# Token stage of an audio tower: the pointwise convolution an iteration later, four accumulator banks for it and two for the convolution, the second norm one iteration behind the first

## The reference, cut to what matters

```python
# token stage, for each of 16 batches: x is 64 channels x 2048
h = conv1d(x, conv_in_w, stride=1, pad=3)                     # 64 -> 128 channels, 7 taps
h = gelu(groupnorm1(h, gn1_w, gn1_b))                         # norm over all of a batch
h = conv1d(h, dw_w, stride=2, pad=2, groups=H) + dw_b         # depthwise, 5 taps, 128 x 1024
h = conv1d(h, pw_w)                                           # pointwise, 128 -> 128
h = gelu(groupnorm1(h, gn2_w, gn2_b))                         # 16 x 128 tokens of 1024
# then h + attention(layernorm(h)), then + mixture of low-rank experts on layernorm(...)
```

## Time and profile before

| | |
|---|---|
| median of three runs | 2040.95 us |
| profiled execution | 2044.69 us |
| its span | 2042.9 us |
| PE busy | 1892.5 us, 93% |
| DVE busy | 1321.2 us, 65% |
| ACT busy | 773.2 us, 38% |
| POOL busy | 308.4 us, 15%, all but 83 us of it before 421 us |

### The profile page before, as it was taken

The page is one execution under the profiler, slowest core; times in us unless marked ns, Lnnn a source line. Parts: engine busy times, 40 slices in busy tenths (PEclk is TensorE's granted clock), DMA queues, the critical chain, the costliest instruction groups (busy, mean ns, idle before and its releaser), DMA issues. The chain is left out here.

```text
span 2042.9 us, 32412 instructions
## 1 busy us (share of the span) xinstructions
PE 1892.5 (93%) x11538; PEld 1029.6 (50%) x11538; DVE 1321.2 (65%) x2742; ACT 773.2 (38%) x2020; POOL 308.4 (15%) x596
## 2 busy tenths in 40 slices
PE   4898898559999999999999999999999999859999
PEld 2344444335555555555555555555555555425554
DVE  4678777436666666666666666666666666555554
ACT  3454554233333334433333433333343333332221
POOL 2376675300000000000000000000000000033332
PEclk9899999679999999999999999999999999979999
DMA  5244342332222322232222222223222222243332
GB/s 143 52 86 96 81 95 65 76 91 51 58 58 59 76 56 53 58 76 59 58 58 55 73 58 58 58 58 75 55 55 58 40 39 39 39 138 80 80 82 73
DMA packets 305609, 138.87 MB, mean 68 GB/s; under 512 B 295088, under 2 KB 295344, under 8 KB 303408
## 3 DMA queue, kind: packets, MB, share of 16 engines
q1 hardware_dynamic: 301136, 108.35, 24.8%
q10 hardware_dynamic: 4320, 28.51, 4.0%
HBM read 56.07 MB, written 8.39 MB: 32 GB/s over the span
## 5 line engine op out<-in xcount | busy, mean ns | idle before, releaser
L1031 PE MATMUL out_ps<-m_h,ot_h 128*128 128x512 f16 x1024 | 389.4, 380 | 1.7 <-DVE ot_l L835 1.7
L1032 PE MATMUL out_ps<-m_l,ot_h 128*128 128x512 f16 x1024 | 389.0, 380 | 0.0
L1033 PE MATMUL out_ps<-m_h,ot_l 128*128 128x512 f16 x1024 | 388.9, 380 | 0.0
L756 ACT ACTIVATE qp_h<-qp_ps 128x512 f16<-128x512 f32 x126 | 75.3, 597 | 492.6 <-PE qp_ps L966 492.6
L812 ACT ACTIVATE prob<-s_ps,nmx 128x128 f32<-128x128 f32 x512 | 181.3, 366 | 207.3 <-DVE nmx L905 207.3
L885 DVE SCALAR_TENSOR_TENSOR resid<-out_ps,resid 128x512 f32<-128x512 f32 x256 | 176.1, 688 | 97.1 <-PE out_ps L1033 97.1
L835 DVE SCALAR_TENSOR_TENSOR qp_l<-qp_ps,qp_h 128x512 f16<-128x512 f32 x126 | 87.2, 692 | 234.5 <-ACT qp_h L756 234.5
L1221 POOL MEMSET fpower<- 128x1 f32 x1 | 0.1, 99 | 1392.4 <-POOLq L674 1392.4
L966 PE MATMUL qp_ps<-lat,wp_h 128*128 128x512 f16 x756 | 205.6, 381 | 0.0
L1033 PEld LDWEIGHTS out_ps<-m_h,ot_l 128*128 128x128 f16 x1024 | 100.4, 98 | 121.6 <-issue 1.4
L1031 PEld LDWEIGHTS out_ps<-m_h,ot_h 128*128 128x128 f16 x1024 | 100.5, 98 | 110.5 <-DVE ot_l L835 2.7
(11 more groups left out here) (217 smaller groups left out, 3861.3 us busy)
## 6 DMA issues: line engine op xcount, KB each, us to landing
wide<-heads_in ACTq DMA_DIRECT2D x30, 928.0 KB, 4.7
wide<-x_in SPq DMA_DIRECT2D x30, 512.0 KB, 6.5
tower_out<-result SPq DMA_DIRECT2D x16, 512.0 KB, 2.6
stage<-wb_in SPq DMA_DIRECT2D x8, 512.0 KB, 8.3
resid<-wqk_in SPq DMA_DIRECT2D x1, 2304.0 KB, 11.6
zt<-z SPq DMA_TRANSPOSE x128, 2.4
turned<-halves SPq DMA_TRANSPOSE x128, 3.0
wide<-heads_in SPq DMA_DIRECT2D x2, 928.0 KB, 4.6
```

The lines of the kernel that those rows point to most:

```text
L756: act.activation(out, src, ACT.Copy, scale=scale).then_inc(done, 1)
L1031: pe.matmul(out_ps[hf][:, :], ot_h[:, h, :], m_h[:, at], start=h == 0, stop=False)
L1032: pe.matmul(out_ps[hf][:, :], ot_h[:, h, :], m_l[:, at], start=False, stop=False)
L1033: last = pe.matmul(out_ps[hf][:, :], ot_l[:, h, :], m_h[:, at], start=False, stop=h == HEADS - 1)
```

## The change

- The pointwise product gets a lag of its own, PW = 2. It moves from the end of PE's iteration to the place behind the statistics matmul, ahead of chunk 1. HID, PROJ and TAIL become 3, 4 and 5; LOW is merged into TAIL. The number of iterations stays the same.
- Banks: two for the convolution's chunks, four for the pointwise product (two batches of two halves). `stat_ps` becomes four columns of the second convolution bank, so the statistics matmul waits until that bank's chunk has been copied, and chunk 1 waits until the statistics have been copied.
- Tap 0 of the depthwise convolution goes from DVE to ACT, behind the first Gelu.
- ACT's order: chunks 0, 1 and 2 are copied, then the second Gelu, the first Gelu, tap 0, `x_high`, chunk 3, the latents' high parts, the squares.
- POOL's order: group norms, latent scales, layer norm, and `x_low` last.
- DVE's order: the pointwise product's statistics ahead of the taps, the latents' low parts at the end of the iteration.
- SP's order: the next x is loaded ahead of the latents' transposing DMAs.

```diff
-    AHEAD, MID, HID, PROJ, TAIL, LOW = -1, 1, 2, 3, 4, 5
+    AHEAD, MID, PW, HID, PROJ, TAIL = -1, 1, 2, 3, 4, 5
-        conv_ps = [pb("conv_ps0"), pb("conv_ps1"), pb("conv_ps2")]
-        stat_ps = pb("stat_ps")
-        pw_ps = [pb("pw_ps0"), pb("pw_ps1")]
+        conv_ps = [pb("conv_ps0"), pb("conv_ps1")]
+        pw_ps = [[pb(f"pw_ps{b}{hf}") for hf in range(2)] for b in range(2)]
+        stat_ps = conv_ps[1][:, 0:4]
...
@@ sync, body @@
-                if ok(LOW):
-                    b = i - LOW
+                if ok(-2) and i >= -1:
+                    sp.wait_ge(x_hi, i + 2)
+                    sp.wait_ge(x_lo, i + 2)
+                    load(i + 2, 0, XW, x_loaded)
+                if ok(TAIL):
+                    b = i - TAIL
                     sp.wait_ge(lat_lo, b * 2 + 2)
...
@@ scalar, body @@
+                if ok(TAIL) and i - TAIL + PROJ >= B:
+                    squares(i - TAIL)
                 if ok(0):
                     copy_y1(i, p, 0)
-                if ok(AHEAD):
-                    x_high(i - AHEAD)
-                if ok(0):
                     copy_y1(i, p, 1)
-                if ok(MID):
-                    act.wait_ge(gn_step, i * GN_STEPS)
-                    need(act, dw_step, (i - MID) * DW_TAPS, B * DW_TAPS)
-                    act.activation(g1[:, DW_PAD:DW_PAD + T], y1[1 - p][:, :], ACT.Gelu, bias=c12[:, 1:2],
-                                   scale=c12[:, 0:1]).then_inc(gelu1_done, 1)
-                if ok(0):
                     copy_y1(i, p, 2)
                 if ok(HID):
...
+                if ok(MID):
+                    b = i - MID
+                    act.wait_ge(gn_step, i * GN_STEPS)
+                    need(act, dw_step, b * DW_TAPS, B * DW_TAPS)
+                    act.activation(g1[:, DW_PAD:DW_PAD + T], y1[1 - p][:, :], ACT.Gelu, bias=c12[:, 1:2],
+                                   scale=c12[:, 0:1]).then_inc(gelu1_done, 1)
+                    act.wait_ge(gelu1_done, b + 1)
+                    need(act, pw_done, b * 2, 2 * B)
+                    act.activation(dw[:, :], g1[:, 0:2 * D:2], ACT.Identity, bias=params[:, 5:6],
+                                   scale=params[:, 0:1]).then_inc(dw_step, 1)
+                if ok(AHEAD):
+                    x_high(i - AHEAD)
                 if ok(0):
                     copy_y1(i, p, 3)
...
@@ gpsimd, body @@
-                if ok(AHEAD) and i >= 0:
-                    x_low(i - AHEAD)
                 if ok(TAIL):
                     latent_scales(i - TAIL)
                 if ok(HID):
                     layer_norm(i - HID)
+                if ok(AHEAD) and i >= 0:
+                    x_low(i - AHEAD)
...
@@ vector, body @@
-                if ok(LOW):
-                    latents_low(i - LOW)
...
                     stats1(i, p, 1)
-                if ok(MID):
-                    for k in range(DW_TAPS):
-                        tap(i - MID, k)
+                if ok(PW):
+                    b = i - PW
+                    for hf in range(2):
+                        dve.wait_ge(pw_done, b * 2 + (hf + 1))
+                        dve.bn_stats(bn2[:, hf, :], pw_ps[b % 2][hf][:, :]).then_inc(bn2_done, 1)
+                    wait_apart(dve, dve_passed, (bn2_done, b * 2 + 2), (stat_done, i))
+                    mean_and_square(st2_ready, b, st[:, 2:4], bn2[:, :, :])
                 if ok(HID):
...
+                if ok(0):
+                    stats1(i, p, 2)
...
+                if ok(MID):
+                    for k in range(1, DW_TAPS):
+                        tap(i - MID, k)
+                if ok(0):
                     stats1(i, p, 3)
...
+                if ok(TAIL):
+                    latents_low(i - TAIL)
...
@@ tensor @@
-                need(pe, y1_copied, i * 4 + (c - 2), 4 * B)
+                need(pe, y1_copied, i * 4 + (c - 1), 4 * B)
+                if c == 1:
+                    need(pe, s_copied, i, LAST + HID)
...
                     need(pe, s_copied, i - 1, LAST + HID)
-                    pe.matmul(stat_ps[:, 0:4], keep["mean_mat"][:, :], st[:, :], start=True, stop=True
+                    need(pe, y1_copied, i * 4, 4 * B)
+                    pe.matmul(stat_ps, keep["mean_mat"][:, :], st[:, :], start=True, stop=True
                               ).then_inc(stat_done, 1)
+                if ok(PW):
+                    pointwise(i - PW)
                 if ok(0):
                     conv(i, p, 1)
...
                 if ok(PROJ):
                     project(i - PROJ)
-                if ok(MID):
-                    pointwise(i - MID)
```

More of the change, by code:

```diff
@@ L179, in token_phase @@
         HEAD = 2 * CHUNK + 8
-        lags = list(range(AHEAD, LOW + 1))
+        lags = list(range(AHEAD, TAIL + 1))
         block = ctx.enter_context(nc.Block())
@@ L260, in copy_y1 @@
                     need(act, gelu1_done, i - 1, B)
-                act.activation(y1[p][:, c * CHUNK:(c + 1) * CHUNK], conv_ps[(i * 4 + c) % 3][:, :], ACT.Copy
+                act.activation(y1[p][:, c * CHUNK:(c + 1) * CHUNK], conv_ps[(i * 4 + c) % 2][:, :], ACT.Copy
                                ).then_inc(y1_copied, 1)
@@ L264, in copy_y1, with squares @@
                     weights_high("wqk", QUARTERS[c])
+            def squares(b):
+                act.wait_ge(proj_done, b + 1)
+                need(act, rms_step, b * RMS_STEPS, B * RMS_STEPS)
+                need(act, ss_done, b * 2, 2 * B)
+                act.activation(junk[:, :], q_ps[:, 0:QR], ACT.Square, scale=UN * QR ** -0.5,
+                               accum_out=ss[:, 0:1]).then_inc(ss_done, 1)
+                act.wait_ge(ss_done, b * 2 + 1)
+                act.activation(junk[:, 0:KVR], kv_ps[:, 0:KVR], ACT.Square, scale=UN * KVR ** -0.5,
+                               accum_out=ss[:, 1:2]).then_inc(ss_done, 1)
             def body(i, p, ok):
@@ L295, in body @@
                     for hf in range(2):
-                        act.activation(resid[:, b * D + hf * CHUNK:b * D + (hf + 1) * CHUNK], pw_ps[hf][:, :],
-                                       ACT.Gelu, bias=c12[:, 3:4], scale=c12[:, 2:3]).then_inc(gelu2_done, 1)
+                        act.activation(resid[:, b * D + hf * CHUNK:b * D + (hf + 1) * CHUNK],
+                                       pw_ps[b % 2][hf][:, :], ACT.Gelu, bias=c12[:, 3:4], scale=c12[:, 2:3]
+                                       ).then_inc(gelu2_done, 1)
+                if ok(MID):
[10 more added lines that the diff above has]
+                    x_high(i - AHEAD)
                 if ok(0):
@@ L308, in body @@
                                    ).then_inc(kc_hi, 1)
[L309 to L318, removed]
+                if ok(PROJ) and i < B:
+                    squares(i - PROJ)
             act.wait_ge(zeroed, ZEROED)
-            pipeline(act, body, -1, lags, LOW)
+            pipeline(act, body, -1, lags, TAIL)
         @block.gpsimd
@@ L432, in tap, with hid_low @@
             def tap(b, k):
[L434 to L443, removed]
+                dve.wait_ge(dw_step, b * DW_TAPS + k)
+                dve.scalar_tensor_tensor(out=dw[:, :], in0=g1[:, k:k + 2 * D - 1:2],
+                                         scalar=params[:, k:k + 1], in1=dw[:, :],
+                                         op0=ALU.mult, op1=ALU.add).then_inc(dw_step, 1)
+            def hid_low(b):
+                dve.wait_ge(hid_hi, b + 1)
+                need(dve, hid_turned, b * 16, B * 16)
+                low(hid2[:, D:2 * D], hid[:, :], LN_S, hid2[:, 0:D], hid_lo)
             def take_latents(b):
@@ L489, in body @@
                     need(dve, gn_step, (i - 1) * GN_STEPS, (LAST + HID) * GN_STEPS)
-                    dve.tensor_copy(s[:, :], stat_ps[:, 0:4]).then_inc(s_copied, 1)
+                    dve.tensor_copy(s[:, :], stat_ps).then_inc(s_copied, 1)
                 if ok(PROJ):
[L492 to L495, removed]
-                if ok(LOW):
-                    latents_low(i - LOW)
+                    hid_low(i - PROJ)
                 if ok(TAIL):
@@ L531, in body @@
                     mean_and_square(st1_ready, i, st[:, 0:2], bn1[:, :, :])
-                if ok(MID):
[L533 to L538, removed]
+                if ok(TAIL):
+                    latents_low(i - TAIL)
             dve.wait_ge(zeroed, ZEROED)
             dve.wait_ge(w_loaded["params"], 16)
-            pipeline(dve, body, -1, lags, LOW)
+            pipeline(dve, body, -1, lags, TAIL)
         @block.tensor
@@ L560, in conv @@
                         lo = c * CHUNK + 2 * m
-                        last = pe.matmul(conv_ps[(i * 4 + c) % 3][:, :], w[:, m, :], x[p][:, lo:lo + CHUNK],
+                        last = pe.matmul(conv_ps[(i * 4 + c) % 2][:, :], w[:, m, :], x[p][:, lo:lo + CHUNK],
                                          start=n == 0, stop=n == 3 * PAIRS - 1)
@@ L567, in pointwise @@
                 pe.wait_ge(dw_step, b * DW_TAPS + DW_TAPS)
-                need(pe, gelu2_done, b * 2, 2 * B)
```

(3 more changed lines are left out.)

19 lines of the change are left out of this document (6 added, 13 removed).

## The result

| | before | after |
|---|---|---|
| median | 2041.53 us (four runs beside it) | 2098.49 us (2096.22 to 2100.0) |
| ratio | | 1.0277 [1.0259, 1.0295] |
| profiled execution, its span | 2044.69 us, 2042.9 us | 2098.74 us, 2096.9 us |
| copy of the statistics by DVE, i = 3 | 78.25 us | 79.79 us |
| the same, i = 15 | 337.19 us | 378.57 us |

The change costs 57.0 us by the medians and 54.0 by the two spans. By the copies of the statistics, which every iteration has once, 1.5 of the 54 us arose in the head, 39.8 in the twelve steady iterations (24.90 us each instead of 21.58) and 13.0 in the tail. What follows the first attention matmul took 1621.8 us, before 1622.2, which is no loss. One run of the kernel before among those beside the last two experiments took 7984 us and is left out of every figure.

A forecast was written before the change was run, and what follows sets the result against it. No engine was full; a ring of dependencies across engines set 21.64 us an iteration. Twelve iterations at +3.0 (ring 1.7, clock 1.3), head +2 and tail +8 gave +46 us: 2087 us by the median, range 2060 to 2104.

The forecast's parts named there:

- the likeliest case: Whole kernel: the forecast's own band of 2076 to 2098 us, given a chance of 0.62.
- The ring: Steady iteration, dependency chain from one statistics matmul to the next across the engines: 23.3 us instead of 21.64, +1.7.
- The clock: Steady iteration: PE's wait inside chunk 0 lets its granted clock fall, costing 1.3 us, between nothing and 1.7.
- The head: Earliest iterations: first norms and splits run in another order, +2 us, between -2 and +4.
- The tail: From the last steady iteration to the first attention matmul: 83.6 us before, +8 us expected.
- The extra pass: Tail: one more pass of hid, transpose, projection and statistics without convolution, some 16 us.
- the last leg: End of the tail: the last hid no longer waits behind the squares, saving 5.2 us.
- (1): Steady iterations: x_low and taps run beside one another, ring of 19.4 us, about 2021 us in all; chance 0.08.
- (4): Steady iterations: the moves cancel, x_low half hidden, ring about 21.5 us, 2045 us in all; chance 0.04.
- (2): Steady iterations: ring as forecast, clock falls lie in the wait or don't come; +30, 2071 us; chance 0.15.
- (3): After each PE wait the clock stays low twice as long, 1.3 us more an iteration; +64, 2105 us; chance 0.11.
- the 22.9: Steady iteration: ring in us if tap 0 stayed on DVE at 0.81 us instead of 1.24 on ACT.

The follow-up runs named there:

- e3: The changed kernel with sixteen matmuls without effect added per iteration ahead of chunk 0's own, filling PE's wait: 2066.84 us, ratio 1.0120.
- e2: The changed kernel with POOL running x_low between latent scales and layer norm, so that it comes up among the taps: 2098.49 us, ratio 1.0280.
- e6: The changed kernel with tap 0 put back on DVE: 2095.26 us, ratio 1.0268.
- b1: The kernel before with tap 0 alone moved to ACT behind the first Gelu: 2033.74 us, ratio 0.9958; measured again, 2032.08 us, 0.9949.
- b3: The kernel before with tap 0 on ACT, chunk 2's copy before the first Gelu, its statistics before the taps, rotary additions behind them: 2027.24 us, ratio 0.9927.
- e1: The changed kernel with the split of x (x_high on ACT, x_low on POOL) back in its earlier place: 2037.44 us, ratio 0.9974.

## Why the prediction was right, and where it was not

The forecast was 2087 us, the result 2098.49. It lies in the range, 0.5 us above the likeliest case's own (2076 to 2098). The path and the waits were as foretold; the sizes of three terms were not, and that the errors partly cancel is luck. Point by point:

**The mechanism held.** x_low starts with the end of the last tap and PE waits for it inside chunk 0, by 4.28 and 4.52 us where 4.7 stood in the prediction; the layer norm's steps take 1.13 us beside the taps; ACT's second Gelu follows the copy of chunk 2, and its copy waits for PE, not for POOL.

**The ring was 0.5 us too long.** e3 shows it without the clock, counted from a statistics matmul at 234.66 (the `s` copy at 235.06 less 0.4). Its steps against those of the prediction: copy of chunk 2 begins at +7.4 (7.4), first Gelu +9.2 (9.2), tap 0 +11.4 (11.4), taps +12.7 (12.7), their end +18.0 (17.9), x_low ends +21.8 (22.4), average iteration 22.76 (23.3). The one step that failed is that between taps and x_low. The last held step of the layer norm ended with the last tap, not 0.5 us behind it, and x_low followed it at once, without the hand-over of 0.25. Tap 0 on ACT, for which no row was at hand, took 1.31 to 1.34 us: the neighbour of equal size (1.24) was the right one to lean on, not the double for the stride.

**The clock was under-sized, 2.14 us an iteration and not 1.3.** The argument was that part of a fall would lie inside the wait. Hardly any of it did: the clock was 1.00 and 0.93 in the two waits and 0.54 in the 6.74 us behind the second. Nor was it always one stretch of 3.4 us; the falls at 153, 252 and 351 us lasted 6.8, and the one at 95 us 13.7. In all 63.2 us were at half clock between the two copies, 5.3 an iteration, against 0.6 in e3; half of the difference, 2.35, is near the 2.14 that e3 gave back. The two errors point in opposite ways, 0.5 too much and 0.84 too little, so 24.6 stood for 24.90, 36 us for 39.8: the closeness of the two is luck in part.

**The head** came out at 1.5 us for 2. **The tail** at 13.0 for 8. The extra pass, from one `s` copy to the next, took 19.5 us where 16 had been put down, and the earlier part of the drain became 0.7 us shorter instead of 3; the last leg gave 5.8 us back, for 5.2. SP's timeline in the extra pass shows a part of it:

```profile
419.05 0.58 SPq L221 DMA_DIRECT2D wide<-heads_in  x1
419.73 5.17 SPq L202 DMA_TRANSPOSE ht<-hid_hl  x1
```

The pass's transposing DMA of `ht` came up right behind a load for the attention stage on the same queue and took 5.17 us; the one before it, at 402.47, took 1.80, and the two after it, at 437.49 and 452.13, 1.92 and 1.32. The one at 381.31, also right behind such a load, took 4.79. No run moves the load, so that these 3.4 us are its doing is not shown.

**The rivals.** (1), x_low and taps side by side, fell with e2: the taps stand still for x_low's length, and x_low waits for the tap under way. (4), x_low half hidden with a ring of 21.5 us, fell with x_low's place behind the last tap and the 22.76 us that are left without the clock. (2), the ring right and the clock without cost, gave 2071 us; e3, which takes the falls away by force, gives 2066.84, so its total was near and its condition did not hold; within that total the ring was too long and the tail too short. (3), a clock low for twice as long, had 1.3 us more an iteration than the forecast; the clock took 0.84 more. The truth lies between forecast and rival 3, nearer to the latter.

**Two rules that had been weighed.** The Trainium skill, "SBUF — State Buffer", section "Who interferes with whom", had been drawn on for what no row of before showed, a large POOL operation between two taps. e2 bears it out: 8.95 us for 5.25. The sum by it, an iteration as long as with x_low last, holds too (25.14 and 24.90). The Trainium skill, "Perfetto Trace Analysis", section "Optimizing Scalar/DVE Operations", was right on the instruction (0.80 us on DVE, 1.31 on ACT) and the 22.9 worked out beside it was not borne out: e6's iteration is that of after, because the layer norm's steps took over. In b1 the offload paid although DVE was not full, since DVE's instruction had taken 2.44 us under x_low.

What stays open: whether the load made that DMA slow, why the drained iterations gained 0.7 us rather than 3, and whether b3 could keep its 20.22 us with the later pointwise product as well, which was not tried.

## What to carry to other kernels

Treat a large operation on GpSimd and a chain on VectorE that hold each other up as one serial resource, and put the large one where the chain isn't ready: here the place in the queue of one 3.8 us subtraction was worth 4.2 us in every iteration, more than all the rest of the change (0.9 us). Before an operation is moved to the end of a queue, follow its result to the first reader that stands in order on another engine, and before it is moved to the front, follow what is queued behind it. A wait that recurs on TensorE can cost more than its length, here another 2.1 us an iteration in clock, and a pipeline made a stage deeper pays for it at its end, 9 us in this case (e1's tail against that of before).

## What the runs showed of the hardware that was not expected

- An operation's size says nothing of how long it is held: beside x_low a 128x1 operation on DVE took 3.02 us (0.22 alone), and two 128x64 additions took 3.97 us (0.34 to 0.35 alone).
- Filling TensorE's wait with sixteen superfluous matmuls made the kernel 31.7 us faster.
- In the two waits shown the clock was 1.00 and 0.93, and it was low when the work came back: the fall hit the work, and at most 0.6 us of the idle time that preceded it.
- A transposing DMA right behind a load on its queue took 5.17 us at the end of the stage. In the steady part, where the load of x now stands three DMAs ahead of it, it took 3.92 and 5.25 us (at 232.23 and 256.78); in the kernel before, where that load was issued after it, 1.94 and 1.89 (at 209.81 and 231.46). Cause and effect were not tried.
